# A two-stage kernel (attention, then routed experts): the last two batches written as one program, expert weights loaded inside the loop, and each batch's steps in another order

## The reference, cut to what matters

```python
x = x + tanh(g_xattn) * xattn(layernorm(x), ctx, ctx, w_q, ..., b_o)   # 16 heads of 16, softmax
x = x + tanh(g_ffn) * ffn(layernorm(x), conf_w, conf_b, gate_w, up_w, down_w, wealth)

# ffn: 8 experts, 2 for each token
bids = sigmoid(x @ conf_w.T + conf_b) * wealth
top_bids, selected = top_k(bids, 2)
combine = sum(one_hot(selected, 8) * softmax(top_bids)[..., None], axis=2)
output = einsum("ebsh,bse->bsh", [(silu(x @ g.T) * (x @ u.T)) @ d.T for each expert], combine)
```

## Time and profile before

| | |
|---|---|
| runs, median (lowest to highest) | 1084.11 us (1083.93 to 1085.11) |
| profiled execution, its own time | 1083.07 us |
| its span, first to last instruction | 1081.4 us |
| mean granted TensorE clock | 0.969 |
| PE busy | 1001.3 us (93%) |
| DVE, ACT, POOL busy | 610.8, 502.0, 366.3 us |
| start of batch 2, of batch 14 (first V product on PE) | 98.27, 398.00 us |
| first product of the last batch's heads (`turn_heads` of 15) | 443.19 us |
| first product of the expert loop | 483.24 us |

### The profile page before, as it was taken

How to read it: one execution, slowest core, us unless ns; L and a number is a source line. 1 busy time by engine, 2 the same in 40 slices (tenths; PEclk the granted TensorE clock), 3 DMA queues, 4 the chain that set the end, 5 groups by cost and what they waited for, 6 DMA issues and landing times.

```text
span 1081.4 us, 25127 instructions
## 1 busy us (share of the span) xinstructions
PE 1001.3 (93%) x8750; PEld 855.2 (79%) x8750; DVE 610.8 (56%) x1519; ACT 502.0 (46%) x796; POOL 366.3 (34%) x439
## 2 busy tenths in 40 slices
PE   5789999999999997759999999999999999999993
PEld 4556777777777765448999999999799999999993
DVE  3556777777777776455544444444554444444452
ACT  4366777777777774334323232332433323233321
POOL 1124555555555552443322212121332212122121
PEclk8799999999999999869999999999999999999997
DMA  8000111111111119258712111121262212121211
GB/s 254 27 22 22 43 45 47 41 41 41 43 51 58 41 39 371 77 182 323 256 25 40 25 35 35 25 37 23 42 229 49 37 23 40 20 40 23 37 35 17
DMA packets 48338, 77.30 MB, mean 71 GB/s; under 512 B 8616, under 2 KB 42152, under 8 KB 44456
## 3 DMA queue, kind: packets, MB, share of 16 engines
q0 software_dynamic: 18080, 50.15, 16.7%
q1 hardware_dynamic: 30216, 26.62, 8.3%
HBM read 52.09 MB, written 24.40 MB: 71 GB/s over the span
## 4 chain that ended last, share of the span: by engine, by line
PE 81%; ACT 5%; issue 4%; DVE 3%; POOL 3%; DMA 1%; SPq 1%; POOLq 1%; ACTq 0%; DVEq 0%
PE gate L1485 17%; PE up L1485 17%; PE down L1499 11%; PE down L1501 6%; PE pv L590 4%; PE scores L579 4%; PE misc L486 4%; PE scores L540 3%; PE maxps L554 2%; PE misc L513 2%; PE misc L522 2%; POOL K_rest L1204 2%; ACT probs L771 1%; PE misc L624 1%; PE turned L1468 1%
## 5 line engine op out<-in xcount | busy, mean ns | idle before, releaser
L1937 POOL DMA_INDIRECT out<-y,token x64 | 100.9, 1577 | 424.8 <-DVE y L1806 323.8
L1696 ACT ACTIVATE silu<-gate 128x512 f32<-128x512 f32 x128 | 76.8, 600 | 281.6 <-PE up L1485 281.6
L984 DVE TENSOR_REDUCE max_neg<-maxps 128x4 f32<-128x1024 f32 x128 | 156.5, 1222 | 60.2 <-PE maxps L554 60.2
L1485 PE MATMUL gate<-x_hi,w_split 128*128 128x256 f32 x1024 | 185.0, 282 | 2.0 <-DVE x_lo L1772 1.6
L1797 DVE TENSOR_TENSOR h<-silu,up 128x512 f32<-128x512 f32 x128 | 88.1, 688 | 174.8 <-ACT silu L1696 174.8
L1499 PE MATMUL down<-w_split,h_hi 128*128 128x512 f32 x512 | 185.9, 398 | 0.0
L1485 PE MATMUL up<-x_hi,w_split 128*128 128x256 f32 x1024 | 184.4, 282 | 0.0
L771 ACT ACTIVATE probs<-scores 128x1024 f32<-128x1024 f32 x124 | 127.2, 1026 | 80.5 <-PE scores L579 79.5
L1485 PEld LDWEIGHTS gate<-x_hi,w_split 128*128 128x128 f32 x1024 | 149.4, 189 | 5.5 <-issue 2.7
L1485 PEld LDWEIGHTS up<-x_hi,w_split 128*128 128x128 f32 x1024 | 148.8, 189 | 0.0
L1501 PE MATMUL down<-w_split,h_lo 128*128 128x256 f32 x512 | 144.1, 281 | 0.0
(11 more groups left out here) (204 smaller groups left out, 1586.3 us busy)
## 6 DMA issues: line engine op xcount, KB each, us to landing
stage<-gate_up_T POOLq DMA_DIRECT2D x20, 1024.0 KB, 8.1
stage<-down_T POOLq DMA_DIRECT2D x10, 1024.0 KB, 11.1
xg<-dispatched SPq DMA_DIRECT2D x34, 272.0 KB
ctxT<-ctxT SPq DMA_DIRECT2D x17, 256.0 KB, 2.8
x_all<-x SPq DMA_DIRECT2D x16, 256.0 KB, 5.2
out<-x_all SPq DMA_DIRECT2D x16, 256.0 KB, 2.2
dispatched<-pads SPq DMA_DIRECT2D x4, 272.0 KB, 3.6
dispatched<-pads POOLq DMA_DIRECT2D x4, 272.0 KB, 4.3
```

Source lines behind the costliest of these rows:

```text
L984: V.tensor_reduce(to, maxps[:], AX.X, ALU.max, negate=True).then_inc(s["max_taken"], 1)
L1485: last = mm(bank[:, i, :], into_inner(w, pair, mat)[:, c, cols], r[:, c, :], start=m == 0, stop=m == len(terms) - 1)
L1696: nc.scalar.activation(silu[pair % 2][:], gate[pair % 2][:], ACT.Silu).then_inc(s_silu, 1)
L1937: pool.indirect_dma_start(out, bass.IndirectOffsetOnAxis(token[:, t:t + 1], axis=0), y[:, t, :], None, compute_op=ALU.add).then_inc(s_adde ...
```

## The change

- **Last two batches.** Batches 14 and 15 (C and Z) are no longer two calls of `body`: each engine has one `last_two`, in which the heads, logits and routing of 12 to 14 (A, B, C) are placed by hand among the scores of 14 and 15.
- **Weights.** Experts 0 and 1 are loaded inside the loop, behind batches 5 and 9 (the loop of POOL is cut in three); `load_ahead` stays, in `last_two`, ahead of the scatter of batch 12.
- **Order of a batch.** PE: the score of pairs 5 to 7 ahead of the maxima product of the same pair, the query product in two halves between them, `turn_x2` behind value product 2, `turn_maxima` ahead of value product 3 and `logits` behind it; Q0 goes to `maxps` instead of `scores`. ACT: `read_k` and `norm_x` earlier, `norm_x2` later. DVE: `read_logits` moves to the next batch's start, `positions` ahead of the sixth maxima reduction.
- **Ranks.** Five small products become two, with `macc` held in two halves; `positions` has 13 links instead of 14.
- **First rows.** PE turns the first expert rows straight from `xg`; POOL's copy of them is gone, and ACT reads the turned rows in two halves.

```diff
-        FULL = ["V", "TO0", "TO1", "K", "TN", "WO", "TX", "RK", "Q", "TX2", "LG", "MT"]
+        FULL = ["V", "TO0", "TO1", "K", "TN", "WO", "TX", "RK", "Q", "TX2", "MT", "LG"]
...
+        LAST_TWO = ["V", "TO0", "TO1", "TN", "MT", "WO", "RK", "next TO0", "next TO1", "next TN", "next WO", "TX2", "LG", "KNOWN",
+                    "next TX2", "next RK", "next LG"]
...
-        def over_batches(eng, body):
+        def over_batches(eng, body, last_two, loads=()):
...
-            with eng.Fori(1, BATCHES // 2 - 1) as i:
-                for b, par in ((i * 2, 0), (i * 2 + 1, 1)):
-                    body(b, par, full_use(b), True, True, True, True)
-            body(BATCHES - 2, 0, ITER14, False, True, True, True)
-            body(BATCHES - 1, 1, ITER15, False, False, True, True)
+            cuts = (1, *(3 + 2 * n for n in range(len(loads))), BATCHES // 2 - 1)
+            for n, (first, end) in enumerate(zip(cuts, cuts[1:])):
+                with eng.Fori(first, end) as i:
+                    for b, par in ((i * 2, 0), (i * 2 + 1, 1)):
+                        body(b, par, full_use(b), True, True, True, True)
+                if n < len(loads):
+                    loads[n]()
+            last_two()
...
 # PE, ranks
-                for t in range(QT):
-                    mm(use.bank("RK")[:, t, 0:EXPERTS], before[:], m12[:, t, :], start=True, stop=False)
...
+                mm(use.bank("RK")[:, :, 0:EXPERTS], before[:], m12[:], start=True, stop=False)
+                mm(use.bank("RK")[:, :, 0:EXPERTS], ones[:], macc[:], start=False, stop=True).then_inc(s["misc_written"], 1)
...
 # PE, body
                 weigh(b, par, 1)
+                score(b, par, 5)
                 max_of_next(5)
-                score(b, par, 5)
                 if ahead:
-                    project_q(use)
+                    project_q_half(0, use)
                 score(b, par, 6)
+                max_of_next(6)
+                if ahead:
+                    project_q_half(1, use)
+                score(b, par, 7)
+                max_of_next(7)
+                weigh(b, par, 2)
                 if back:
                     turn_x2(b - 1, 1 - par, use)
-                max_of_next(6)
-                score(b, par, 7)
-                weigh(b, par, 2)
-                max_of_next(7)
                 stack_ahead("K1")
+                if nxt:
+                    turn_maxima(b + 1, use)
+                weigh(b, par, 3)
                 if back:
                     logits(use)
-                if nxt:
-                    turn_maxima(b + 1, use)
                 stack_ahead("Q0")
-                weigh(b, par, 3)
                 stack_ahead("Q1")
...
 # PE, last_two
+                weigh(C, 0, 2)
+                scores_and_maxima(7)
+                turn_maxima(Z, END)
+                attn_out(END)
+                weigh(C, 0, 3)
+                ranks(A, END)
+                score(Z, 1, 0)
...
+                attn_out(NEXT_BACK)
+                score(Z, 1, 4)
+                turn_x2(B, 1, END)
+                score(Z, 1, 5)
+                weigh(Z, 1, 1)
+                logits(END)
+                known_counts(END)
+                score(Z, 1, 6)
+                turn_x2(C, 0, NEXT_BACK)
+                score(Z, 1, 7)
+                weigh(Z, 1, 2)
+                END.read(pe, "KNOWN")
+                ranks(B, NEXT_BACK)
+                weigh(Z, 1, 3)
+                logits(NEXT_BACK)
...
 # ACT, body
                 exps(b, 2)
+                if ahead:
+                    read_k(b + 2, use)
                 if back:
                     read_whole(oT[:], "TN", use)
                 exps(b, 3)
+                read_pv(b, 0)
                 if ahead:
-                    read_k(b + 2, use)
                     norm_x(b + 2)
                 exps(b, 4)
...
 # DVE, second_choice and positions
-                V.tensor_tensor(m12[:], m1[:], m2[:], ALU.add).then_inc(s["masks_ready"], 1)
+                V.tensor_tensor(m12[:], m1[:], m2[:], ALU.add).then_inc(s["masks_made"], 1)
...
+                V.tensor_tensor(macc[:, 1, :], macc[:, 0, :].bitcast(fp32), m12[:, 0, :].bitcast(fp32), ALU.add).then_inc(s["masks_ready"], 1)
...
-                link = chain(dve, "rows_chain", 14, b, behind=1)
+                link = chain(dve, "rows_chain", 13, b, behind=1)
...
 # DVE, body
                 max_of_next(4)
-                max_of_next(5)
                 if late:
                     positions(b - 2, par, use)
+                max_of_next(5)
                 max_of_next(6)
                 max_of_next(7)
-                if back:
-                    read_logits(b - 1, use)
                 if nxt:
                     read_maxima(b + 1, use)
...
 # POOL
+            def last_two():
+                scale_x2(B)
+                pool.wait_ge(s["shifted"], Z * (16 * HPP) + 16 * HPP)
+                pool.wait_ge(s["x2_stored"], 16 * C)
+                load_ahead(pool)
+                scatter(A, 0)
+                scale_x2(C)
+                scatter(B, 1)
...
+            over_batches(pool, body, last_two, [lambda: load_weights(0), lambda: load_weights(1)])
```

More of the change, by code:

```diff
@@ L277, in written @@
             def written(self, eng, what):
-                eng.wait_ge(s["misc_written"], self.before + (self.order.index(what) + 1))
+                eng.wait_ge(s["misc_written"], self.before + (self.order.index(self.of + what) + 1))
             def read(self, eng, what):
@@ L287, in attention_stage @@
         STACKS = ["K0", "Q0", "K1", "Q1"]
+        BESIDE = "Q0"
         def units_before(b):
@@ L309, in home @@
             return scores[:]
+        beside = maxps[:].rearrange("p u t s -> p (u t) s")
         def first_stack_unit(b, what):
@@ L479, in turn_x, with half_of @@
                 turn(xn, "TX", use)
+            def half_of(weights, source, what, use, o):
+                for c in range(HC):
+                    last = mm(use.bank(what)[:, o, :], weights[:, c, o * P:(o + 1) * P], source[:, c, :], start=c == 0, stop=c == HC - 1)
+                return last
             def project(weights, source, what, use):
@@ L539, in stack @@
                             r = slice(half * STACK, (half + 1) * STACK)
-                            last = mm(scores[:, half * QT + i, :], picks[f"{what} {part}"][r, i, :], source[what][r, c, :],
+                            last = mm(to[:, half * QT + i, :], picks[f"{what} {part}"][r, i, :], source[what][r, c, :],
                                       start=part == "high", stop=part == "rest")
@@ L680, in stack_ahead @@
                 def stack_ahead(what):
-                    if ahead:
-                        stack(b + 2, what[0], int(what[1]), unit(b, what))
+                    if ahead and what == BESIDE:
+                        stack(b + 2, what[0], int(what[1]), None, beside)
+                    elif ahead:
+                        stack(b + 2, what[0], int(what[1]), unit(b, what) - (1 if UNITS[UNITS.index(what) - 1] == BESIDE else 0))
                 if isinstance(b, int) and b < 2:
@@ L869, in stack_ahead @@
                     if ahead:
-                        read_stack(par, what[0], int(what[1]), unit(b, what))
+                        read_stack(par, what[0], int(what[1]), unit(b, what), beside if what == BESIDE else None)
                 exps(b, 0)
```

204 lines of the change are left out of this document (143 added, 61 removed).

## The result

The changed kernel is **slower**, by 1.9%: 1106.21 us median (1104.32 to 1108.13) against 1084.59 of the kernel before beside it, a ratio of 1.0192 (95% interval 1.0172 to 1.0211). The forecast was 1081.0, with a range from 1068 to 1087. The profiled execution took 1104.32 us, its span 1102.6.

A forecast was written before the change was run, and what follows sets the result against it. PE's list of steps was taken to set the loop (busy 24.31 of 24.87 us). Terms +4.2 - 2.3 + 0.3 - 5.2 = -3.0 against 1083.07 gave 1080.1, with the median 1.04 above: 1081.0 us, range 1068 to 1087.

The forecast's parts named there:

- The wait that it priced: Loop batch, PE ahead of the seventh maxima product: a new wait of about 1.1 us for DVE; batch +0.35.
- K0 no longer waited for POOL: Loop batch, PE: K0 comes at 335.66 instead of 336.15, -0.5, with no wait for POOL before it.
- rival B: `positions` in the loop: thirteen register instructions cost +0.65 to +1.05 a batch, the whole say 1087; chance 0.16.
- PE's order is untouched: Loop batch up to the output projection at 332.04: PE's order unchanged, so DVE's residual starts at 334.19 as before.
- the later end of POOL's query split: Loop batch: POOL's query split ends later, but this vanishes in PE's wait for DVE; no cost.
- A: Loop: PE keeps setting it, each batch gains up to 0.8 instead of losing 0.35; whole 1067; chance 0.2.
- my bounds of -0.8 to +0.65: Change per loop batch: -0.8 if DVE keeps up, +0.65 with the whole register cost; +0.35 taken.
- The last two batches: Batches 14 and 15: turn of the maxima and scores of 15 earlier, batch 15 at 19.8; together -5.2 (-9.4 to -1.3).
- rival C: Last two batches: scatter behind the load holds the layernorm of 14, clock falls, 1.3 gained, whole 1085; chance 0.16.
- Batches 0 and 1: First two batches, without `positions`: -1.5 and -0.8, together -2.3 (-3.2 to -1).
- The tail and the experts: From the last batch's heads through routing, scatter and re-reading, and the experts behind: unchanged, 0.
- The 2 us by which a load might delay the next scale: Weight loads in the loop: POOL delays the next layernorm's scale by at most 2 us, mostly covered; +0.3 (0 to 3).

The follow-up runs named there:

- e11: Changed kernel with load_ahead in the last two batches behind the scatter of 13, not ahead of that of 12: 1102.60 us, ratio 1.0150.
- e6: Changed kernel with POOL's scatter of batch 12 and the second layernorm's scale of 14 ahead of load_ahead: 1108.78 us, ratio 1.0214.
- e2: Changed kernel with DVE's positions again between the sixth and seventh maxima reductions: 1098.30 us, ratio 1.0111.
- e4: Changed kernel with DVE adding the first half of the running count behind the fourth maxima reduction, not at the end of second_choice: 1099.06 us, ratio 1.0134.
- e5: Changed kernel with the edits of e2, e3 and e4 together: 1104.55 us, ratio 1.0180.
- e9: Changed kernel with the three edits of e5, and on POOL the context split and the bias ahead of the scatter: 1086.56 us, ratio 1.0010.
- e3: Changed kernel with ACT reading the query ahead of the exponential of pair 7, as in the kernel before: 1094.72 us, ratio 1.0079.

## Why the prediction was wrong

- **The wait that it priced was there, at its price.** PE waited 1.08 for DVE ahead of the seventh maxima product (1.1 forecast); from DVE's residual to that product it took 6.53 (351.11 to 357.64; 6.6 forecast), and from there to the batch's end 7.97 (7.8 forecast). K0 no longer waited for POOL. `positions` lasted 1.97 up to the next reduction with its register instructions and one link fewer, the 1.97 that was forecast: rival B's extra price was not paid, and no row gives the 0.06 us that it took as the upper price of one such instruction.
- **The step that failed** is the sentence that the batch up to the output projection stays as it was ("PE's order is untouched, so DVE's residual starts ... as before"), with the one that the later end of POOL's query split vanishes. The residual came 12.84 us into the batch instead of 10.82: +2.0 of the +2.2 that a batch lost on average. Of this the third maxima reduction, behind the key product, is 1.36 later (7.87 against 6.51), second choice up to the fourth reduction takes 1.28 more (3.83 against 2.55, the stretched addition), less 0.62 of slack ahead of the residual, which is used up. The walk followed one batch forward and treated its own end as harmless. But ACT's query read was now behind the exponential of pair 7, and that behind the new wait of PE; POOL's scatter and context split hang on it, and they end in the next batch. A wait of 1.1 us could hide the tenths that I put into it only if nothing behind it came round again.
- **No rival had it either.** A asked whether PE stays the bound, B looked for the price in the register instructions; that several engines close a ring, and that a moved addition meets POOL, was in none. The +2.18 a batch lay outside my bounds of -0.8 to +0.65, and they were bounds on terms that I had, not on the one that was missing.
- **The last two batches: mechanism right, one term mis-sized.** The turn of the maxima came 4.5 us earlier (16.55 into batch 14 instead of 21.09), the scores of 15 came 5.0 earlier. PE's wait for the second layernorm of 14, which I named, was 8.0 and not 3 to 4. I put the scatter behind the load at 9 us from issue to landing, the time of a weight transfer; it landed 14.2 us after the load's first issue (443.54 to 457.73), 12.1 after its own first call (445.61). Batch 15 took 24.9 against 19.8, at clock 0.79, and gave all of it back: rival C, in a run where the loop hid it. e11 shows the gain that was there (41.02 against 45.19).
- **Batches 0 and 1.** -4.0 against -2.3; but e6 and e11, the same code up to batch 14, entered the loop at 97.2 and 97.3, not 94.26. So this term is known to about 3 us, from one profile of the kernel before, and its sign alone is as forecast. The tail and the experts were as taken.
- **Weights and small slips.** The 2 us by which a load might delay the next scale rested on no row; behind the loads POOL was 0.6 later, and those two batches were the shorter ones. The sum as written gives 1081.1, the lower bound for batch 15 comes to 15.8 from its own figures and not 15.6, and 0.029 is the shortest of the four register moves shown (median 0.032). None of this bears on the miss.

The third and fourth reductions of the kernel before, in the batch that began at 323.37:

```profile
329.88 1.23 DVE L984 TENSOR_REDUCE max_neg<-maxps 128x4 f32<-128x1024 f32 x1 [0.44 <-PE maxps L554]
...
332.43 1.23 DVE L984 TENSOR_REDUCE max_neg<-maxps 128x4 f32<-128x1024 f32 x1
```

Shown by runs: that the batch hung on the ring and not on positions alone (e2 to e4), the stretched steps (e4, e5 against e9), the load in front of the scatter (e6, e11). Argued from the traces alone: the shorter ring that e2 and e3 fall back on, and that the shorter batches 6 and 10 owe it to POOL's delay by the weight loads. Not tried: each of the change's other moves by itself (Q0 in `maxps`, the two rank products, the loads in the loop).

## What to carry to other kernels

When PE's list is full to 0.5 us of 25, follow a delay round: through every engine that is handed its product, into the next iteration, until it reaches its own start, and compare that ring with PE's list. Each small instruction that moves on DVE needs a look at what POOL reads at that time, and after each repair a new look, since a shorter ring shifts the phase. A large transfer should be issued neither ahead of a small one that someone waits for on the same queue (the scatter here) nor right behind it on another queue (the first rows in e6).

## What had not been expected of the hardware

An addition on 128x8 took 1.17 us and a 128x16 scalar step 1.27, seven times their usual time, when they met a subtraction of POOL. And in two batches of e5 (8 and 12) the granted clock fell to a mean of 0.94 inside the loop, where it was 1.00 in the batches shown around them: the products of the key took 0.63 each instead of 0.40, the lower of the two levels (1.2 instead of 2.4 GHz), right behind a wait of PE of 1.41 for DVE, and the batch took 29.3, with two steps of `second_choice` stretched besides (0.58 and 1.19 in batch 12). Batches with the same wait kept the clock, so what decided it stays open:

```profile
366.27 0.50 PE L583 MATMUL maxps<-keys,queries 48*128 48x256 f32 x4 [1.41 <-DVE max_neg L1094]
...
367.18 0.63 PE L540 MATMUL misc<-ctx_rest,wk_high 128*128 128x256 f32 x2
```
